# Cross attention in the third layer: value and output weights multiplied in an earlier stage, and the weighing done in f32r with high and low parts

## The chip, the core and the metric

One core of one Trainium2 chip runs the whole program, in one launch. The metric is the time on the device in microseconds (us), lower is better. Besides the timed runs there is one profiled execution; starts and durations below are from it, counted from the start of its span. The engines are TensorE (PE; its weight loads are PEld), VectorE (DVE), ScalarE (ACT), GpSimd (POOL) and SyncE (SP, which only issues transfers here).

## The reference, cut to what matters

The reference is a stack of transformer-like layers on 4 sequences of 256 tokens and 256 channels. The change touches two of its parts, the feed-forward part of the second layer (three 8-bit products with a GELU between them) and this cross attention of the third layer:

```python
q = (hidden_states @ Wq).reshape(B, Sq, H, D)            # B 4, Sq 256, H 16, D 128
k = (encoder_hidden_states @ Wk).reshape(B, Skv, H, D)   # the context has 128 channels
v = (encoder_hidden_states @ Wv).reshape(B, Skv, H, D)
q = rmsnorm(q, gq)
k = rmsnorm(k, gk)
scores = einsum('bqhd,bkhd->bhqk', q, k) * scale
attn = softmax(scores, axis=-1)
out = einsum('bhqk,bkhd->bqhd', attn, v)
return out.reshape(B, Sq, H * D) @ Wo
```

## The kernel before

The kernel keeps the residual `x_res` in SBUF and runs one stage after another. Every stage ends with a barrier of all engines. Within a stage each engine has its own instruction list in fixed order, and semaphores tie the lists together.

`l1_ffn` is the feed-forward stage of the second layer. Its main loop has 16 iterations n. PE makes two 128x512 products (`up`), ACT takes one of them and applies the GELU (`take`, L2691 and L2693), and DVE takes the other and multiplies (`product`, L2719 and L2724). ACT (`square`, L2344 to L2348), DVE and POOL then round the result to 8-bit values. `downward` runs behind it for half of the tokens at a time. `Norm` and `Turned` normalise and transpose the input ahead of the loop.

`l2_cross` is the changed stage. It never forms the values v. For each head h it multiplies the value and output weights into one 128x256 matrix, `wvo[:, h, :]`, and works as out = (attn · context) · wvo. Its main loop is a list of steps (it, s), with s from 0 to 15. In step (it, s) head s of sequence it - 1 goes through the pipeline, and the same step projects the keys and queries of sequence it (`pieces`): keys in s 0 to 3, queries in s 3 to 10, sums of squares and means in s 11, turned keys in s 12 to 15. The products of `wvo` (`outw`, L2978 on PE, L3067 on ACT) were pieces of pass it = 0, s 4 to 11; their inputs were loaded by `at_sp` after the stage's first barrier. I call a run of 16 steps with the same `it` a pass: pass 0 only prepares, passes 1 to 3 do both, and pass 4 only works on heads. Head number m = 16(it - 1) + s is what the steps are about:

```python
score(m)            # PE L2988, two f32 matmuls of 256 columns
turn_probs(m - 2)   # PE L2997, four f32 transposes
weigh(m - 3)        # PE L3008, two f32 matmuls of 256 columns
out_product(m - 4)  # PE L3019, the same with wvo; then the pieces of the step
```

On DVE a step is `largest(m)` (the row maximum, L3094, then the small bias for the exponential, L3096), `take_probs(m - 2)` (the copy out of PSUM, L3102), `invert(m)` (L3106), and then what the pieces need: copies of keys (L3120), of turned keys (L3157), `rescale` (L3149), sums. On ACT it is `exponent(m)` (two exponentials and the reads of their sums, L3046), `copy_out(m - 3)` (L3053), and for queries a copy and a square (L3061, L3063). On POOL it is `normalise(m)` (L3205), and in s 1 to 4 also `square` (L3201). `exponent(m)` waits for the bias of head m, `invert(m)` for its exponentials, `normalise(m)` for the reciprocal, and the bank pair 6 and 7 of PSUM alternates over all pieces, so a piece waits until the piece two before it has been taken.

In the profile one f32 matmul of the program shows as two PE records.

Of the kernel before, what the change touches and what calls it, by code (L numbers as in the profile page):

```python
# [2624 lines left out]
def l1_ffn(k):  # L2625
# [5 lines left out]
    with ExitStack() as cx:  # L2631
        sb = k.buffers(cx, "l1f_")
        w8, x8 = sb("w8", [P, 6144], BF16), sb("x8", [P, 2, TOK], F8)
        k.load("l1f", w8[:, :], k.kept8)
# [50 lines left out]
        def at_act():  # L2685
# [178 lines left out]
def l2_cross(k):  # L2864
# [16 lines left out]
    def pieces(b, s):
# [14 lines left out]
    def bank_free(*u):  # L2896
# [12 lines left out]
        return kt_sb(8 * b + i + 1) if kind == "turn" else vo_sb(i + 1)  # L2909

    with ExitStack() as cx:
        sb = k.buffers(cx, "l2x_")
# [20 lines left out]
        pr, pT, oT = sb("probs", [P, 3, 2, S]), sb("pT", [P, 2, 2, S]), sb("oT", [P, 2, S])  # L2933

        def at_pe():
            def piece(kind, b, i):
# [29 lines left out]
                elif kind == "turn":  # L2966
# [6 lines left out]
                else:  # L2973
                    if i == 0:
                        pe.wait_ge(*vo_in(2))
                    pe.wait_ge(*bank_free(kind, b, i))
                    for a in range(2):
                        last = pe.matmul(out[:, a * D:(a + 1) * D], wv[:, 2 * i + a, :], wo[:, 2 * i + a, :], start=True, stop=True)  # L2978
                    last.then_inc(*vo_ps.tick())
# [59 lines left out]
        def at_act():  # L3039
# [720 lines left out]
```

## Time and profile before

| | us |
|---|---|
| median of 3 runs | 2517.75 |
| lowest and highest | 2515.58, 2519.55 |
| the profiled execution's own time | 2513.59 |
| its span in the trace | 2512.4 |
| PE busy | 2084.8 (83%) |
| DVE busy | 1549.1 (62%) |
| ACT busy | 1086.3 (43%) |
| POOL busy | 1075.8 (43%) |
| `l1_ffn`, issue of its weights; main loop | 1242.7; 1250.6 to 1322.5 |
| `l2_cross`, first load to last statistics | 1674.6 to 2044.9 |

A busy share is an average over all stages. What the change does is to be read in the two stages that it touches, from which engine the others wait for there. The page's PE clock row is in tenths of full speed, and matmul ends are modelled, so for PE the distance from one start to the next tells more than a duration.

### The profile page before, as it was taken

Reading aid. Unit: us, or ns where it says so; the run is one execution under the profiler, and the core shown is the slowest. Engines: PE = TensorE matmul, PEld = TensorE weight load, DVE = VectorE, ACT = ScalarE, POOL = GpSimd, SP = SyncE. Lnnn points to the kernel's source line nnn. Section 1 sums busy time; section 2 is a strip of 40 time slices with the busy share of each in tenths; the row PEclk is TensorE's granted clock in tenths of the full one; section 3 lists DMA queues with packets and bytes.
Section 4 is the critical chain, followed back from the end, with each engine's and each line's share of the span. In section 5 each row is a group of like instructions: output and inputs, shape, how many; then the busy total and the mean of one; then the engine's idle time right before and its main releaser. Section 6 shows DMA issues by size and latency. Waiting matters only on the chain. (4 is left out here: it accounts for less than half of the span.)

```text
span 2512.4 us, 35632 instructions
## 1 busy us (share of the span) xinstructions
PE 2084.8 (83%) x12866; PEld 1427.6 (57%) x12866; DVE 1549.1 (62%) x2880; ACT 1086.3 (43%) x2193; POOL 1075.8 (43%) x1101
## 2 busy tenths in 40 slices
PE   5667769999966999968748888877999988898877
PEld 2333346666745999944514444545777765555445
DVE  6877755545455777757685555544456555556546
ACT  3245636455533544534271355532444434432433
POOL 2776707556647777647352233331223222231000
PEclk8766689999987999989859789888999999989788
DMA  4222210000005555430101000020000000112000
GB/s 146 70 61 61 60 43 20 24 13 12 10 23 186 183 181 180 156 128 1 50 1 39 3 3 3 3 110 0 1 1 1 1 1 2 36 42 107 2 1 17
DMA packets 49869, 124.53 MB, mean 50 GB/s; under 512 B 5632, under 2 KB 18432, under 8 KB 47520
## 3 DMA queue, kind: packets, MB, share of 16 engines
q1 hardware_dynamic: 48160, 118.07, 14.7%
q0 software_dynamic: 1536, 4.20, 0.5%
q8 instruction: 104, 1.70, 0.3%
q14 instruction: 69, 0.57, 0.1%
HBM read 105.07 MB, written 16.12 MB: 48 GB/s over the span
## 5 line engine op out<-in xcount | busy, mean ns | idle before, releaser
L1846 POOL TENSOR_SCALAR l0f_probs<-l0f_probs,l0f_tot 128x128 f32<-128x128 f32 (+1 forms) x256 | 202.6, 809 | 121.9 <-DVE l0f_tot L1793 121.6
L236 PE MATMUL ps<-kb 128*128 128x512 bf16 x524 | 149.7, 432 | 55.9 <-PEq L239 55.9
L3205 POOL TENSOR_TENSOR l2x_probs<-l2x_probs,l2x_rc 128x512 f32<-128x512 f32 x64 | 66.5, 1039 | 256.2 <-DVE l2x_rc L3106 256.2
L1308 DVE TENSOR_REDUCE l2a_a_max<-ps 128x6 f32<-128x768 f32 x128 | 119.5, 954 | 87.3 <-PE ps L1160 86.7
L1364 POOL TENSOR_SCALAR_AFFINE_SELECT l2a_a_probs<-l2a_a_probs 128x256 f32<-128x256 f32 (+1 forms) x192 | 88.3, 484 | 170.3 <-ACT l2a_a_probs L1270 147.9
L2064 PE MATMUL ps<-l0f_xh,l0f_wh 128*128 128x256 f32 x480 | 145.9, 304 | 0.0
L2181 POOL TENSOR_TENSOR l0f_wl<-l0f_raw,l0f_wh 128x1024 fp32r<-128x1024 f32 x60 | 142.1, 2388 | 0.0
L1717 ACT ACTIVATE l0f_probs<-ps,l0f_neg 128x128 f32<-128x128 f32 (+1 forms) x256 | 104.5, 425 | 78.6 <-DVE l0f_neg L1783 78.5
L2065 PE MATMUL ps<-l0f_xl,l0f_wh 128*128 128x256 f32 x480 | 136.0, 283 | 0.0
L2066 PE MATMUL ps<-l0f_xh,l0f_wl 128*128 128x256 f32 x480 | 136.0, 283 | 0.0
L3046 ACT ACTIVATE l2x_probs<-ps,l2x_neg,l2x_rs 128x256 f32<-128x256 f32 x128 | 71.1, 559 | 146.1 <-DVE l2x_neg L3096 146.1
L236 PEld LDWEIGHTS ps<-kb 128*128 128x128 bf16 x524 | 52.5, 106 | 124.8 <-issue 88.9
L701 DVE TENSOR_TENSOR_SCAN l1x_h<-l1x_dA,l1x_dBu 128x512 f32<-128x512 f32 x64 | 117.2, 1870 | 7.6 <-ACT l1x_dA L688 7.6
L719 POOL TENSOR_TENSOR l1x_y<-l1x_y,l1x_hc 128x512 f32<-128x512 f32 x64 | 80.8, 1284 | 87.6 <-DVE l1x_hc L710 87.6
L2077 PE MATMUL ps<-l0f_raw_d,l0f_gf 128*128 128x256 f32 x480 | 113.3, 379 | 0.0
L1007 POOL TENSOR_TENSOR l0x_y<-l0x_y,l0x_hc 128x512 f32<-128x512 f32 x64 | 80.3, 1275 | 44.5 <-DVE l0x_hc L980 44.3
L1308 DVE TENSOR_REDUCE l0a_max<-ps 128x4 f32<-128x1024 f32 x64 | 77.7, 1214 | 28.4 <-PE ps L1155 27.8
L2077 PEld LDWEIGHTS ps<-l0f_raw_d,l0f_gf 128*128 128x128 f32 x480 | 88.8, 190 | 9.9
L2064 PEld LDWEIGHTS ps<-l0f_xh,l0f_wh 128*128 128x128 f32 x480 | 92.3, 192 | 2.5
L2065 PEld LDWEIGHTS ps<-l0f_xl,l0f_wh 128*128 128x128 f32 x480 | 92.3, 192 | 1.1
L2066 PEld LDWEIGHTS ps<-l0f_xh,l0f_wl 128*128 128x128 f32 x480 | 92.1, 192 | 0.0
L1270 ACT ACTIVATE l2a_a_probs<-ps 128x1024 f32<-128x1024 f32 x64 | 65.7, 1027 | 58.9 <-PE ps L1187 58.4
(722 smaller groups left out, 5786.4 us busy)
## 6 DMA issues: line engine op xcount, KB each, us to landing
l0f_raw<-in_e_l0f SPq DMA_DIRECT2D x60, 512.0 KB, 4.1
l0x_bc<-scratch_bc SPq DMA_DIRECT2D x32, 512.0 KB, 4.8
l0f_raw_d<-in_e_l0f SPq DMA_DIRECT2D x60, 256.0 KB, 3.2
scratch_rows<-zero SPq DMA_DIRECT2D x1, 3840.0 KB, 19.0
l0f_xb<-scratch_rows SPq DMA_DIRECT2D x15, 256.0 KB, 3.0
scratch_results<-l0f_yb SPq DMA_DIRECT2D x15, 256.0 KB, 2.3
l2f_ew<-in_e_l2f SPq DMA_DIRECT2D x8, 384.0 KB, 3.1
l2f_raw<-in_w_l3f SPq DMA_DIRECT2D x1, 2304.0 KB, 10.3
```

What stands on the lines that cost most here:

```text
L236: self.pe.matmul(bank, self.identb, self.kb[:, 0:512], start=True, stop=True)
L701: k.dve.tensor_tensor_scan(self.row(self.h, d), self.row(self.dA, d), self.row(self.dBu, d), 0.0, ALU.mult, ALU.add).then_inc(*self.state. ...
L719: k.pool.tensor_tensor(yd, yd, self.row(self.hc, d), ALU.add).then_inc(*self.summed.tick())
L1308: dve.tensor_reduce(M[:, 2 * half:2 * half + 2, j, :], src.rearrange("p a (c n) -> p a c n", c=NB_), AX.X, ALU.max).then_inc(*unit_max.tick())
L1364: last = pool.affine_select(part, part, [[0, m], [1, P]], ALU.is_ge, 0.0, base=0, channel_multiplier=-1)
L1717: last = act.activation(pr[:, u % 4, a, r], ps[:, 2 * (u % 2) + a, r], ACT.Exp, scale=scale, bias=neg[:, u % 4, qt, a:a + 1], accum_out=to ...
L1846: last = pool.tensor_scalar(pr[:, u % 4, a, r], pr[:, u % 4, a, r], tot[:, u % 4, qt, a:a + 1], None, ALU.mult)
L2064: pe.matmul(out, hi, xh[:, j % 2, c, :], start=c == 0, stop=False)
L2065: pe.matmul(out, hi, xl[:, j % 2, c, :], start=False, stop=False)
L2066: last = pe.matmul(out, lo, xh[:, j % 2, c, :], start=False, stop=c == 1)
L2077: last = pe.matmul(ps[:, 4 + j % 2, q * D:(q + 1) * D], gf[:, n % 3, f * BLOCK + q * P:f * BLOCK + (q + 1) * P], raw_d[:, n % 6, f * D:(f ...
L2181: pool.tensor_tensor(wl[:, n % 3, :], raw[:, n % 4, :], wh[:, n % 3, :].bitcast(F32), ALU.subtract).then_inc(*w_lo.tick())
```

## The change

Three things. First, `wvo` becomes a buffer that is allocated before `l1_ffn`. That stage now loads the value and output weights (1 MB and 2 MB, behind its own weights on SP), and PE multiplies them in iterations 1 to 8 of its loop (`out_weights`), while ACT takes the results in iterations 2 to 9 (`take_out_weights`). The pieces `outw` and the two loads leave `l2_cross`. Second, the weighing product is made of six f32r matmuls instead of two f32 ones: high context by high probabilities, high by low, and low by high, for each half of the keys. Third, for this the turned probabilities are taken in two parts: ACT copies the high part out of PSUM (`high_probs`), and DVE, which used to copy, subtracts the high part from PSUM to get the low one. The context is split once, by ACT and POOL in pass 0.

```diff
@@ l1_ffn
         k.load("l1f", w8[:, :], k.kept8)
+        wv, wo = sb("wv", [P, 16, P]), sb("wo", [P, 16, D])
+        vo_in, vo_ps, vo_sb = k.sig("out0", 16), k.sig("vo_ps"), k.sig("vo_taken")
+        k.sp.dma_start(wv[:, :, :], k.dram["g_l2x"][:, 6144:8192].rearrange("p (h c) -> p h c", c=P)).then_inc(*vo_in.tick())
+        k.sp.dma_start(wo[:, :, :], k.dram["g_l2x"][:, 8192:12288].rearrange("p (h n) -> p h n", n=D)).then_inc(*vo_in.tick())
+        landed = vo_in.now()
...
+                elif t == 0:
+                    pe.wait_ge(*vo_sb(8))
...
+            def out_weights(i):
+                if i == 0:
+                    pe.wait_ge(*landed)
+                if i >= 2:
+                    pe.wait_ge(*vo_sb(i - 1))
+                for a in range(2):
+                    last = pe.matmul(ps[:, 6 + i % 2, a * D:(a + 1) * D], wv[:, 2 * i + a, :], wo[:, 2 * i + a, :], start=True, stop=True)
+                last.then_inc(*vo_ps.tick())
+
             for n in range(N):
                 up(n)
+                if 1 <= n <= 8:
+                    out_weights(n - 1)
...
+            def take_out_weights(i):
+                act.wait_ge(*vo_ps(i + 1))
+                act.copy(k.wvo[:, 2 * i:2 * i + 2, :].rearrange("p h n -> p (h n)"), ps[:, 6 + i % 2, :]).then_inc(*vo_sb.tick())
+
             for n in range(N + 1):
                 if n < N:
                     take(n)
                 if n:
                     square(n - 1)
+                if 2 <= n <= 9:
+                    take_out_weights(n - 2)
@@ l2_cross
-        return out + ([("outw", 0, s - 4)] if b == 0 and 4 <= s < 12 else [])
+        return out
...
-        xT, wk, wq, wvo = sb("xT", [P, 2, TOK]), sb("wk", [P, 2048]), sb("wq", [P, 2, 2048]), sb("wvo", [P, H, D])
+        xT, wk, wq, wvo = sb("xT", [P, 2, TOK]), sb("wk", [P, 2048]), sb("wq", [P, 2, 2048]), k.wvo
...
-        pr, pT, oT = sb("probs", [P, 3, 2, S]), sb("pT", [P, 2, 2, S]), sb("oT", [P, 2, S])
+        pr, oT = sb("probs", [P, 3, 2, S]), sb("oT", [P, 2, S])
+        ph, pl = sb("pT_h", [P, 2, 2, S], F32R), sb("pT_l", [P, 2, 2, S], F32R)
+        ch, cl = sb("ctx_h", [P, NT, DC], F32R), sb("ctx_l", [P, NT, DC], F32R)
...
-                for kt in range(2):
-                    last = pe.matmul(ps[:, 4, n % 2 * S:(n % 2 + 1) * S], ctx[:, 2 * b + kt, :], pT[:, n % 2, kt, :], start=kt == 0, stop=kt == 1)
+                for i, (c, p, kt) in enumerate([(c, p, kt) for kt in range(2) for c, p in ((ch, ph), (ch, pl), (cl, ph))]):
+                    last = pe.matmul(ps[:, 4, n % 2 * S:(n % 2 + 1) * S], c[:, 2 * b + kt, :], p[:, n % 2, kt, :], start=i == 0, stop=i == 5)
...
+            def high_probs(n):
+                act.wait_ge(*p_ps(n + 1))
+                if n >= 2:
+                    act.wait_ge(*product(n - 1))
+                act.copy(ph[:, n % 2, :, :].rearrange("p k s -> p (k s)"), ps[:, 2 + n % 2, :]).then_inc(*p_hi.tick())
+
...
                 if 0 <= m < N:
                     exponent(m)
+                if 0 <= m - 2 < N:
+                    high_probs(m - 2)
                 if 0 <= m - 3 < N:
                     copy_out(m - 3)
+                if it == 0 and s == 9:
+                    act.wait_ge(*c_in.now())
+                    act.copy(ch[:, :, :], ctx[:, :, :]).then_inc(*c_hi.tick())
...
             def take_probs(n):
-                dve.wait_ge(*p_ps(n + 1))
-                if n >= 2:
-                    dve.wait_ge(*product(n - 1))
-                dve.tensor_copy(pT[:, n % 2, :, :].rearrange("p k s -> p (k s)"), ps[:, 2 + n % 2, :]).then_inc(*p_sb.tick())
+                dve.wait_ge(*p_hi(n + 1))
+                dve.tensor_tensor(pl[:, n % 2, :, :].rearrange("p k s -> p (k s)"), ps[:, 2 + n % 2, :],
+                                  ph[:, n % 2, :, :].rearrange("p k s -> p (k s)").bitcast(F32), ALU.subtract).then_inc(*p_sb.tick())
...
+                if it == 0 and s == 9:
+                    pool.wait_ge(*c_hi(1))
+                    pool.tensor_tensor(cl[:, :, :], ctx[:, :, :], ch[:, :, :].bitcast(F32), ALU.subtract).then_inc(*c_lo.tick())
 
         def at_sp():
-            sp.dma_start(wv, k.dram["g_l2x"][:, 6144:8192].rearrange("p (h c) -> p h c", h=H)).then_inc(*vo_in.tick())
-            sp.dma_start(wo[:, :, :], k.dram["g_l2x"][:, 8192:12288]).then_inc(*vo_in.tick())
@@ build
+        k.wvo = k.buffers(ctx, "l2x_")("wvo", [P, 16, D])
         l1_ffn(k)
```

On ACT, in the last pass of `l2_cross`, the instruction list of before repeats these rows for each head (L3046 is the exponential, `l2x_oT` the copy of the weighed context):

```order
L3046 ACTIVATE l2x_probs,l2x_tot<-ps,l2x_neg,l2x_rs 128x256 [waits s_turned,s_bias]
L3046 ACTIVATE l2x_probs,l2x_tot<-ps,l2x_neg,l2x_rs 128x256
L3053 COPY l2x_oT<-ps 128x256 [waits s_out_ps,s_product]
L3046 ACTIVATE l2x_probs,l2x_tot<-ps,l2x_neg,l2x_rs 128x256 [waits s_turned,s_bias]
L3046 ACTIVATE l2x_probs,l2x_tot<-ps,l2x_neg,l2x_rs 128x256
```

The same place of the changed kernel:

```order
L3063 ACTIVATE l2x_probs,l2x_tot<-ps,l2x_neg,l2x_rs 128x256 [waits s_turned,s_bias]
L3063 ACTIVATE l2x_probs,l2x_tot<-ps,l2x_neg,l2x_rs 128x256
L3070 CAST l2x_pT_h<-ps 128x512 [waits s_product,s_turned]
L3076 COPY l2x_oT<-ps 128x256 [waits s_out_ps,s_product]
L3063 ACTIVATE l2x_probs,l2x_tot<-ps,l2x_neg,l2x_rs 128x256 [waits s_turned,s_bias]
```

The new cast stands behind both exponentials of the step, although it belongs to the head two before theirs.

On DVE at the same place, before:

```order
L3094 TENSOR_REDUCE l2x_mx<-ps 128x2 [waits s_scored]
L3096 SCALAR_TENSOR_TENSOR l2x_neg<-l2x_mx,l2x_rs 128x2 [waits s_v]
L3102 COPY l2x_pT<-ps 128x512 [waits s_product,s_turned]
L3106 RECIPROCAL l2x_rc<-l2x_tot 128x2 [waits s_weighed]
L3094 TENSOR_REDUCE l2x_mx<-ps 128x2 [waits s_scored]
```

And after:

```order
L3114 TENSOR_REDUCE l2x_mx<-ps 128x2 [waits s_scored]
L3116 SCALAR_TENSOR_TENSOR l2x_neg<-l2x_mx,l2x_rs 128x2 [waits s_v]
L3120 TENSOR_TENSOR l2x_pT_l<-ps,l2x_pT_h 128x512 [waits s_x_hi]
L3125 RECIPROCAL l2x_rc<-l2x_tot 128x2 [waits s_weighed]
L3114 TENSOR_REDUCE l2x_mx<-ps 128x2 [waits s_scored]
```

The order is the same; the third instruction now waits for ACT (`x_hi` is the semaphore of the cast), where it had waited for PE.

On PE at the start of the loop of `l1_ffn`, the changed kernel has these rows (before, the rows L2672 stood without those of L2691 between them):

```order
L2672 MATMUL ps<-l1f_x,l1f_w 128x512 [waits s_ld_l1f,barrier_Pool_Activation_PE_DVE_SP_release]
L2672 MATMUL ps<-l1f_x,l1f_w 128x512 x7
L2691 MATMUL ps<-l1f_wo,l1f_wv 128x256 [waits s_out0]
L2691 MATMUL ps<-l1f_wo,l1f_wv 128x256
L2672 MATMUL ps<-l1f_x,l1f_w 128x512 x4
```

Behind the products of iterations 0 and 1 PE now waits for the two new loads (`out0`), and the products of iteration 2 stand behind that wait.

## Rows read from the trace of the kernel before

**Rows 1.** Busy time by engine in stretches of `l2_cross`: setup, one pass, last pass.
```profile
core 0: us, PE busy (x) PEld busy (x) DVE busy (x) ACT busy (x) POOL busy (x), PEclk, DMA share, GB/s
...
1693.80:1713.80 20.00, 18.01 (x77) 13.98 (x78) 0.56 (x1) 9.87 (x20) 0.00 (x0) 1.00 0.00 1
...
1785.80:1869.50 83.70, 81.58 (x404) 64.02 (x403) 48.78 (x94) 35.04 (x100) 24.03 (x20) 1.00 0.00 1
...
1988.70:2042.70 54.00, 53.71 (x281) 46.66 (x279) 28.97 (x70) 25.86 (x85) 16.64 (x16) 1.00 0.00 1
```
**Rows 2.** Timeline of PE, one head of the last pass.
```profile
2012.03 0.60 PE L2997 MATMUL ps<-kf,l2x_probs 128*128 128x128 f32 x4
2012.46 1.03 PE L3008 MATMUL ps<-l2x_pT,l2x_ctx 128*128 128x256 f32 x4
2013.33 1.03 PE L3019 MATMUL ps<-l2x_wvo,l2x_oT 128*128 128x256 f32 x4
2014.19 1.03 PE L2988 MATMUL ps<-l2x_kT,l2x_qT 128*128 128x256 f32 x4
```
**Rows 3.** Timeline of DVE, the same head, and the next maximum.
```profile
2009.20 0.69 DVE L3094 TENSOR_REDUCE l2x_mx<-ps 128x2 f32<-128x512 f32 x1 [0.71 <-PE ps L2988]
...
2009.92 0.16 DVE L3096 SCALAR_TENSOR_TENSOR l2x_neg<-l2x_mx,l2x_rs 128x2 f32<-128x2 f32 x1
...
2011.36 0.17 DVE L3106 RECIPROCAL l2x_rc<-l2x_tot 128x2 f32<-128x2 f32 x1 [0.66 <-ACT l2x_probs L3046]
...
2012.23 0.69 DVE L3094 TENSOR_REDUCE l2x_mx<-ps 128x2 f32<-128x512 f32 x1 [0.70 <-PE ps L2988]
```
**Rows 4.** Timeline of ACT, same head: first exponential, then the copy behind both.
```profile
2010.12 0.56 ACT L3046 ACTIVATE l2x_probs<-ps,l2x_neg,l2x_rs 128x256 f32<-128x256 f32 x1 [1.56 <-DVE l2x_neg L3096]
...
2011.22 0.36 ACT L3053 COPY l2x_oT<-ps 128x256 f32<-128x256 f32 x1
```
**Rows 5.** Timeline of POOL, the same head.
```profile
2011.60 1.04 POOL L3205 TENSOR_TENSOR l2x_probs<-l2x_probs,l2x_rc 128x512 f32<-128x512 f32 x1 [1.99 <-DVE l2x_rc L3106]
```
**Rows 6.** Timeline of DVE, one step that turns keys, pass 1.
```profile
1813.05 0.68 DVE L3094 TENSOR_REDUCE l2x_mx<-ps 128x2 f32<-128x512 f32 x1
...
1815.19 0.17 DVE L3106 RECIPROCAL l2x_rc<-l2x_tot 128x2 f32<-128x2 f32 x1 [0.66 <-ACT l2x_probs L3046]
...
1815.28 1.39 DVE L3157 TENSOR_SCALAR l2x_kT<-ps,l2x_gg 128x512 f32<-128x512 f32 x2
...
1817.72 0.69 DVE L3094 TENSOR_REDUCE l2x_mx<-ps 128x2 f32<-128x512 f32 x1
```
**Rows 7.** Timeline of both engines where a bias meets a POOL instruction.
```profile
1745.98 1.89 POOL L3201 TENSOR_TENSOR l2x_sq<-l2x_k 128x1024 f32<-128x1024 f32 x1
...
1746.71 1.17 DVE L3096 SCALAR_TENSOR_TENSOR l2x_neg<-l2x_mx,l2x_rs 128x2 f32<-128x2 f32 x1
```
**Rows 8.** Groups by line and form, cross and feed-forward stages of the last layer.
```profile
L3594 ACT CAST l3f_xTh<-ps 128x512 fp32r<-128x512 f32 x2 | 1.2, 586 | 4.8 <-PE ps L393 4.8
...
L3598 DVE TENSOR_TENSOR l3f_xTl<-ps,l3f_xTh 128x512 fp32r<-128x512 f32 x4 | 2.5, 684 | 0.2 <-ACT l3f_xTh L3594 0.2
```
**Rows 9.** Timeline of PE, f32r matmuls of 256 columns in the first layer's experts.
```profile
903.57 0.28 PE L2066 MATMUL ps<-l0f_xh,l0f_wl 128*128 128x256 f32 x1
903.69 0.28 PE L2064 MATMUL ps<-l0f_xh,l0f_wh 128*128 128x256 f32 x1
```
**Rows 10.** Timeline of PE, two following query pieces of pass 0.
```profile
1701.07 1.99 PE L2950 MATMUL ps<-l2x_xT,l2x_wq 128*128 128x256 f32 x8 [0.31 <-ACT l2x_sq L3063]
...
1704.24 1.99 PE L2950 MATMUL ps<-l2x_xT,l2x_wq 128*128 128x256 f32 x8 [0.31 <-ACT l2x_sq L3063]
```
**Rows 11.** Timelines of DVE (first) and ACT (second), loop of `l1_ffn`.
```profile
1258.90 0.68 DVE L2719 CAST l1f_ub<-ps 128x512 bf16<-128x512 f32 x1
...
1268.35 0.63 ACT L2344 ACTIVATE l1f_I<-l1f_ab 128x512 f32<-128x512 bf16 x1 [0.78 <-DVE l1f_ab L2724]
```
**Rows 12.** DMA issues of the stage's start, KB each and us to landing.
```profile
l2x_wq<-in_g_l2x SPq DMA_DIRECT2D x1, 2048.0 KB, 9.5
```

More of the change, by code:

```diff
@@ L2872, in l2_cross @@
     scale = 1.0 / math.sqrt(hd)
-    k_in, q_in, vo_in, c_in = k.sig("slab0", 16), k.sig("slab1", 16), k.sig("out0", 16), k.sig("out1", 16)
+    k_in, q_in, c_in = k.sig("slab0", 16), k.sig("slab1", 16), k.sig("out1", 16)
     k_ps, k_sb, q_ps, q_sb, q_sq = k.sig("projected"), k.sig("k_taken"), k.sig("q_ps"), k.sig("q_taken"), k.sig("q_squared")
@@ L2908, in bank_free @@
             return mean(b + 1)
-        return kt_sb(8 * b + i + 1) if kind == "turn" else vo_sb(i + 1)
+        return kt_sb(8 * b + i + 1)
     with ExitStack() as cx:
         sb = k.buffers(cx, "l2x_")
-        xT, wk, wq, wvo = sb("xT", [P, 2, TOK]), sb("wk", [P, 2048]), sb("wq", [P, 2, 2048]), sb("wvo", [P, H, D])
+        xT, wk, wq, wvo = sb("xT", [P, 2, TOK]), sb("wk", [P, 2048]), sb("wq", [P, 2, 2048]), k.wvo
         ctx = sb("ctx", [P, NT, DC])
@@ L2965, in piece @@
                     last.then_inc(*rows_ps.tick())
-                elif kind == "turn":
+                else:
                     pe.wait_ge(*scaled(4 * b + i // 2 + 1))
@@ L2972, in piece @@
                     last.then_inc(*kt_ps.tick())
[L2973 to L2979, printed above, removed]
             def score(n):
@@ L3002, in weigh @@
                 if n == 0:
-                    pe.wait_ge(*c_in.now())
+                    pe.wait_ge(*c_lo(1))
                 pe.wait_ge(*p_sb(n + 1))
@@ L3056, in take_queries @@
                 act.wait_ge(*q_ps(8 * b + i + 1))
-                if b == 1 and i == 0:
-                    act.wait_ge(*vo_ps(8))
                 if b >= 2 and i == 0:
@@ L3063, in take_queries @@
                 act.activation(sq[:, 2 * i:2 * i + 2, :].rearrange("p h s -> p (h s)"), bank("queries", b, i), ACT.Square).then_inc(*q_sq.tick())
-            def take_out_weights(i):
-                act.wait_ge(*vo_ps(i + 1))
-                act.copy(wvo[:, 2 * i:2 * i + 2, :].rearrange("p h n -> p (h n)"), bank("outw", 0, i)).then_inc(*vo_sb.tick())
             def take_root(b):
@@ L3085, in at_act @@
                             take_root(b)
-                        elif kind == "outw":
-                            take_out_weights(i)
             k.root_table()
@@ L3154, in take_turned @@
                     dve.wait_ge(*scored(H * (b - 1)))
-                if b == 1 and i == 0:
-                    dve.wait_ge(*vo_ps(8))
                 dve.tensor_scalar(KT[b % 2][:, 2 * i:2 * i + 2, :].rearrange("p h s -> p (h s)"), bank("turn", b, i), gg[:, 0:1], None, ALU.mult).then_inc(*kt_sb.tick())
@@ L3212, in at_pool @@
                     square(it, s - 1)
+                if it == 0 and s == 9:
+                    pool.wait_ge(*c_hi(1))
+                    pool.tensor_tensor(cl[:, :, :], ctx[:, :, :], ch[:, :, :].bitcast(F32), ALU.subtract).then_inc(*c_lo.tick())
         def at_sp():
-            sp.dma_start(wv, k.dram["g_l2x"][:, 6144:8192].rearrange("p (h c) -> p h c", h=H)).then_inc(*vo_in.tick())
-            sp.dma_start(wo[:, :, :], k.dram["g_l2x"][:, 8192:12288]).then_inc(*vo_in.tick())
             for s in (k_in, q_in, c_in):
                 sp.wait_ge(*s.now())
-            sp.wait_ge(*vo_in.now())
         at_pe()
```

6 lines of the change are left out of this document (2 added, 4 removed).

## The prediction

> **What bounds the kernel now.** The change touches two stages, so I read those, not the whole span. First the busy time by stretch [rows 1]. In one full pass of `l2_cross` PE is busy 81.58 of 83.70 us, in the last pass 53.71 of 54.00, at full granted clock, and DVE about half. By this table PE is the limit. A table of shares hides how close the next limit is, so next I laid the timelines of one head side by side.
>
> In the last pass a head takes 3.03 us from one row maximum to the next [rows 3]. PE needs all of it: weighing starts at 2012.46, the output product at 2013.33, the next score at 2014.19, so 0.86 us for each pair of f32 matmuls, and 0.43 for the transposes [rows 2]. Beside it runs a chain that goes back and forth between DVE and ACT. The maximum starts at 2009.20, the bias at 2009.92 [rows 3], the first exponential at 2010.12, and ACT is free again at 2011.22 [rows 4]. The reciprocal starts at 2011.36 [rows 3]. From the maximum these are 0.72, 0.92, 2.02 and 2.16 us. DVE is then free 0.09 us later, as 1815.19 to 1815.28 shows [rows 6]. So the chain takes 2.25 us, 0.78 less than PE. The copy of the probabilities costs nothing there: DVE makes it while ACT computes exponentials.
>
> In a step that turns keys PE is not the limit even now. Maximum to maximum is 4.67 us, and DVE works through it: 2.14 to the reciprocal, then two turned keys and one rescaling [rows 6]. Any lengthening of the chain is paid there in full.
>
> **Setup: `outw` leaves pass 0.** Query pieces follow each other every 3.17 us, and PE waits at each for the square of the query piece before [rows 10]. With `outw` between them, queries always use the same PSUM bank. Without it they alternate over two, and the pitch becomes PE's own: eight half matmuls at 0.86/4 = 0.216, or 1.73 us. ACT needs less than that for a copy and a square, about 1.2 by the 0.59 of a cast of this form [rows 8]. Six pieces gain 6 x 1.44 = 8.6, and the first wait for the weights (pieces went on at 1693.8, the last sums began at 1713.8 [rows 1]) adds some tenths: **-9.0**. The split of the context is 1024 wide. It stands in step 9, where ACT has 0.5 us to spare per piece, and PE is a full piece ahead; twice the 512-wide cast is 1.2, so it delays one copy by some 0.6 and is caught up by the next. POOL is idle. Price 0; if its cover went, 0.6.
>
> **Weighing on PE.** Six f32r matmuls of 256 columns start 0.12 us apart [rows 9], so 0.72 instead of 0.86: -0.14 per head. It counts only where PE bounds the step, some seven query steps in each of passes 1 to 3: 21 x 0.14 = **-3.0**. If a change of type costs a start, the gain is nothing. The Trainium skill (TensorE: Matmul & The Clock Gate, "Wait — 56ns, not 53.3ns?") gives columns over 2.4 GHz plus about 2.5 ns, measured for bf16, as the distance of two matmuls. That would be 0.109 and a gain of 0.21 per head, -4.4 instead of -3.0. The row has the very type and shape, so its 0.12 stands.
>
> **The high and low parts.** The high part, an ACT cast of 128x512 from PSUM, takes 0.586 us, and the subtraction on DVE, one operand in PSUM, 0.684 [rows 8]. By duration the subtraction only replaces a copy of 0.69. By place it does not. The cast stands behind the exponentials of the step, the subtraction waits for it, and the reciprocal and the next maximum are queued behind the subtraction. So the hidden copy is now in series. The chain from the maximum: 2.02 until ACT is free, 2.61 cast done, 0.03 for the signal, 0.60 until DVE takes the next instruction, reciprocal at 3.24. That is **1.08 us later** than 2.16. The next maximum can start at 3.33.
>
> Bounds: if the cast cost only its pitch, near 0.49, the shift is about 1.0; with one more signal it is 1.2.
>
> Then POOL. Its normalisation starts 0.24 after the reciprocal and takes 1.04 us [rows 5]. The bias is short, 0.16 us, but where one met a POOL instruction it was stretched until that ended: started at 1746.71 against a POOL instruction from 1745.98 for 1.89, it took 1.17 [rows 7]. With the new chain this happens in the last pass at every head: normalisation from 3.48 to 4.52, the next bias due at 3.33 + 0.72 = 4.05, so it ends near 4.7, and a head takes 4.54 - 0.72 = **3.82** instead of 3.03.
>
> Now the places, one by one:
> - last pass: 14 heads x 0.79 = 11.1; the head with the residual addition and the end of the pipeline (cast and subtraction once more) together 1.7: **+12.8**
> - steps that turn keys, and the one behind them (also bound by DVE, since its keys follow the reciprocal): 5 steps x 3 passes x 1.08 = **+16.2**
> - the step that takes the roots, and the one before it, where the chain starts late: some 0.6 per pass, **+2**
> - key steps: the chain, 3.33 + 2 x 0.6 for the keys, just about equals PE. But POOL's 1.89 us square starts when the keys are copied, near 4.7, and the next bias falls into it, as in rows 7. That costs 1.1, twice a pass: **+6.6**
> - query steps: chain 3.33, PE 4.6. The chain is hidden; only the -3.0 counts.
>
> The loop comes to 12.8 + 16.2 + 2 + 6.6 - 3.0 = +34.6.
>
> **`l1_ffn`.** SP issues 3 MB behind the stage's 1.5 MB. A load of 2048 KB, with 1024 KB of another in front of it, landed 9.5 us after its issue [rows 12]. Scaled by 4608/3072 KB that is 14.2 us, and the stage issues at 1242.7: landing near 1257. PE reaches the wait two iterations into a loop that starts at 1250.6, long before. Iteration 2 is queued behind: after the wait four half matmuls and its own four products, 1.7 to 3.4 us by the clock. DVE took its product at 1258.90 [rows 11], so it comes 0 to 3 us late; I take 1.5. The eight copies of 0.59 on ACT: ACT waits 0.78 us for DVE in an iteration [rows 11], so they fit: 0, and 8 x 0.59 = 4.7 without that cover. Term: **+1.5**, bounds 0 and 7.
>
> **Sum.** -9.0 + 34.6 + 1.5 = +27.1 us, so 2513.6 becomes 2540.7 for a profiled execution. That execution was 4.2 us under the median of runs; added to the median, 2517.75 + 27.1 = 2544.9. I say **2545**.
>
> **The rivals.**
> - *The bias does not wait for POOL, or only sometimes.* A head of the last pass takes 3.33, not 3.82 (-6.9), and key steps lose the 6.6: +13.6, 2531. For it: the chain may settle in another phase. Against it: the bias is due 0.5 us after POOL starts, every time. The Trainium skill (SBUF — State Buffer, "Practical consequences") says that a DVE instruction with two SBUF inputs contends with a GpSimd one that reads SBUF, and the loser blocks for the whole instruction. By that rule the wait is no accident; the 1.17 us row agrees. Chance 0.12.
> - *The feed-forward stage pays more.* ACT becomes its limit and the wait for 3 MB is long: +7 instead of 1.5, 2550. For it: the wait comes while the loop fills, when every engine needs PE. Against it: the 0.78 us that ACT has to spare once it runs. Chance 0.14.
> - *Faster: PE stays the limit.* If cast and subtraction hid in the 0.78 us that the chain is shorter than PE, and the turning steps grew no longer, the change keeps -9.0, the 0.14 at all 64 heads (-9.2), and +1.5: -16.7, 2501. It decides at a lengthening of about 0.3 us a step: 15 steps on DVE's path times 0.3, with 1 us elsewhere, make up for what is saved. I forecast 1.08 from measured durations and a fixed order. Chance 0.05.
> - *Gain and loss cancel.* The chain grows by some 0.4 and the net is within 5 us: 2517. Chance 0.03.
>
> **How the numbers follow.** My forecast has 0.66; its own range, from a shift of 1.0 to 1.2 over some 35 steps, 0 to 3 us in `l1_ffn` and 4 us between runs, is 2538 to 2552. Reaching to the two rivals on the slow side gives 2531 to 2554, with some 0.12 outside. A measurement of this kernel tells 0.2% (5 us) from no change. Faster by over that 0.05, within it 0.03, slower 0.92.
>
> **What would show it.** In the changed trace: query pieces of pass 0 some 1.73 us apart and the first row maximum near 9 us earlier within the stage; the subtraction on DVE idle before it, released by ACT's cast; maximum to maximum 3.8 in the last pass and 5.75 in turning steps; biases of 0.6 us instead of 0.16; weighing 0.72 us on PE, with PE idle behind it; the first product of the new pair in `l1_ffn` waiting for a DMA. Wrong would be: 3.0 in the last pass (the cast is hidden), 3.3 (no wait for POOL), or a loop of `l1_ffn` longer by over 4 us.

## The result

The changed kernel takes 2548.68 us (median of 4 runs, 2545.38 to 2554.99), the kernel before 2516.66 us (median of 4 runs beside them). The ratio is 1.0121, 95% interval 1.0095 to 1.0147: by the ratio 30.5 us slower, interval 24 to 37; the medians differ by 32. The forecast was 2545 us, range 2531 to 2554.

The profiled execution took 2545.38 us with a span of 2544.1, against 2513.59 and 2512.4. I cut both spans at the same instructions:

| stretch, from start to start | before | after | difference |
|---|---|---|---|
| `l1_ffn`: main loop to POOL's last product | 65.38 | 67.29 | +1.9 |
| `l2_cross`: first keys to the sums of pass 0 | 32.30 | 23.19 | -9.1 |
| `l2_cross`: first row maximum to the last | 294.29 | 325.72 | +31.4 |
| `l2_cross`: last maximum to the next stage | 11.75 | 12.59 | +0.8 |
| the rest, whose code didn't change | 2108.64 | 2115.33 | +6.7 |

One head of the last pass after the change, the timeline of DVE, ACT and POOL alone (start, us, engine, line, and in brackets the idle time before it and what ended it):

```profile
2035.93 0.58 ACT L3070 CAST l2x_pT_h<-ps 128x512 fp32r<-128x512 f32 x1
2036.54 0.69 DVE L3120 TENSOR_TENSOR l2x_pT_l<-ps,l2x_pT_h 128x512 fp32r<-128x512 f32 x1 [1.75 <-ACT l2x_pT_h L3070]
2037.15 0.15 DVE L3125 RECIPROCAL l2x_rc<-l2x_tot 128x2 f32<-128x2 f32 x1
2037.22 0.67 DVE L3114 TENSOR_REDUCE l2x_mx<-ps 128x2 f32<-128x512 f32 x1
2037.38 1.04 POOL L3222 TENSOR_TENSOR l2x_probs<-l2x_probs,l2x_rc 128x512 f32<-128x512 f32 x1 [2.60 <-DVE l2x_rc L3125]
2037.92 0.52 DVE L3116 SCALAR_TENSOR_TENSOR l2x_neg<-l2x_mx,l2x_rs 128x2 f32<-128x2 f32 x1
2038.47 0.56 ACT L3063 ACTIVATE l2x_probs<-ps,l2x_neg,l2x_rs 128x256 f32<-128x256 f32 x1 [1.69 <-DVE l2x_neg L3116]
2039.57 0.58 ACT L3070 CAST l2x_pT_h<-ps 128x512 fp32r<-128x512 f32 x1
2040.18 0.69 DVE L3120 TENSOR_TENSOR l2x_pT_l<-ps,l2x_pT_h 128x512 fp32r<-128x512 f32 x1 [1.74 <-ACT l2x_pT_h L3070]
2040.79 0.15 DVE L3125 RECIPROCAL l2x_rc<-l2x_tot 128x2 f32<-128x2 f32 x1
2040.86 0.67 DVE L3114 TENSOR_REDUCE l2x_mx<-ps 128x2 f32<-128x512 f32 x1
```

Read it against [rows 3, 4], and against the copy of the turned probabilities in the same head of the kernel before, from its timeline:

```profile
2010.00 0.69 DVE L3102 COPY l2x_pT<-ps 128x512 f32<-128x512 f32 x1
```

Maximum to maximum is now 3.64 us. The copy stood beside ACT's exponentials (2010.12 to 2011.22); the subtraction in its place waits 1.74 us for the cast, which starts when the second exponential is done, and the reciprocal and the next maximum follow at once. POOL starts 0.16 us behind the maximum, and the bias, 0.16 us long before, takes 0.52: it ends at 2038.44, POOL at 2038.42. ACT waits 1.69 us for it.

In the key steps the bias meets POOL's square, as in [rows 7] but now twice in every pass. From the timeline of a pass 2 step:

```profile
1840.71 1.89 POOL L3218 TENSOR_TENSOR l2x_sq<-l2x_k 128x1024 f32<-128x1024 f32 x1
1840.74 0.68 DVE L3114 TENSOR_REDUCE l2x_mx<-ps 128x2 f32<-128x512 f32 x1
1841.45 1.17 DVE L3116 SCALAR_TENSOR_TENSOR l2x_neg<-l2x_mx,l2x_rs 128x2 f32<-128x2 f32 x1
```

The delay goes on to PE, and now and then to its clock. PE's timeline in pass 2, and windows of the same place in passes 1, 2 and 3 (columns as in [rows 1]):

```profile
1845.78 2.62 PE L2976 MATMUL ps<-l2x_xT,l2x_wq 128*128 128x256 f32 x8 [2.59 <-DVE l2x_k L3139]
1848.19 1.91 PE L3007 MATMUL ps<-l2x_kT,l2x_qT 128*128 128x256 f32 x4
```

```profile
1756.00:1760.00 4.00, 4.00 (x20) 3.42 (x19) 1.96 (x3) 1.22 (x3) 0.69 (x1) 0.72 0.00 0
...
1846.00:1850.00 4.00, 4.00 (x13) 3.14 (x13) 3.85 (x5) 1.08 (x2) 2.10 (x2) 0.62 0.00 0
...
1937.00:1941.00 4.00, 3.82 (x22) 3.46 (x23) 3.96 (x6) 1.18 (x2) 2.51 (x2) 1.00 0.02 4
```

Behind its wait of 2.59 us PE was granted 0.62 in pass 2, a part of the time at 1.2 GHz, and made 13 matmuls in 4 us; four of a score took 1.91 instead of 1.03. In pass 3, behind an equal wait but at 2.4 GHz throughout, it made 22. In pass 1 the wait was 3.40 us, and the clock was down behind it too. The step of the long wait and the next took 9.61 and 4.60 us in pass 1, 9.40 and 4.82 in pass 2, 9.06 and 3.46 in pass 3; before, 6.86 and 4.76, then twice 8.07 and 3.36.

Of the 64 biases 23 are longer than 0.23 us after the change, 6 before. Each of the 23 ends 0.02 us behind a POOL instruction. Of the two long ones in the key steps of pass 1 neither is new: the kernel before has both, and [rows 7] shows the first. The page's costliest groups show who pays (busy and mean ns, then idle time before and its releaser):

```profile
L3222 POOL TENSOR_TENSOR l2x_probs<-l2x_probs,l2x_rc 128x512 f32<-128x512 f32 x64 | 66.6, 1040 | 267.9 <-DVE l2x_rc L3125 267.9
L3063 ACT ACTIVATE l2x_probs<-ps,l2x_neg,l2x_rs 128x256 f32<-128x256 f32 x128 | 71.0, 559 | 162.7 <-DVE l2x_neg L3116 162.6
L3120 DVE TENSOR_TENSOR l2x_pT_l<-ps,l2x_pT_h 128x512 fp32r<-128x512 f32 x64 | 44.2, 691 | 108.4 <-ACT l2x_pT_h L3070 108.4
```

The last row is the new wait: 108.4 us over 64 heads, 1.69 each. Most of it is idle time that DVE had anyway, now in another place, so it is not the loss itself; the next section tells what of it is.

In `l1_ffn` the timeline shows the wait for the 3 MB, and the window behind it the clock:

```profile
1258.11 2.07 PE L2691 MATMUL ps<-l1f_wo,l1f_wv 128*128 128x256 f32 x4 [4.24 <-DMA l1f_wo<-in_g_l2x]
1261.08 0.58 ACT L2709 CAST l1f_gb<-ps 128x512 bf16<-128x512 f32 x1 [2.86 <-PE ps L2672]
1261.93 0.69 DVE L2743 CAST l1f_ub<-ps 128x512 bf16<-128x512 f32 x1 [1.57 <-PE ps L2672]
```

```profile
1258.00:1262.00 4.00, 3.89 (x9) 2.43 (x10) 1.07 (x3) 1.11 (x3) 2.53 (x2) 0.50 0.00 0
```

PE comes out of the wait at a granted clock of 0.50, that is 1.2 GHz, and the four matmuls of the fold take 2.07 us. DVE's product of iteration 2 starts 9.94 us into the loop (from 1251.99), before 8.29 (1258.90 [rows 11] less 1250.61): 1.65 later.

### The profile page after: what moved, and what is told of

It is laid out like the page before. It is cut to its first block and busy times, and to the rows that moved or that the text cites. A ratio compares the mean times of both kernels' runs of the same rounds, so it can differ in the third digit from the quotient of the medians.

```text
span 2544.1 us, 35890 instructions
## 1 busy us (share of the span) xinstructions
PE 2078.2 (82%) x12933; PEld 1435.7 (56%) x12994; DVE 1550.9 (61%) x2880; ACT 1116.9 (44%) x2258; POOL 1078.6 (42%) x1102
## 5 line engine op out<-in xcount | busy, mean ns | idle before, releaser
L236 PE MATMUL ps<-kb 128*128 128x512 bf16 x493 | 144.0, 437 | 60.3 <-PEq L239 44.4
L3120 DVE TENSOR_TENSOR l2x_pT_l<-ps,l2x_pT_h 128x512 fp32r<-128x512 f32 x64 | 44.2, 691 | 108.4 <-ACT l2x_pT_h L3070 108.4
```

Of the source, the lines that this page charges most:

```text
L236: self.pe.matmul(bank, self.identb, self.kb[:, 0:512], start=True, stop=True)
```

## The experiments

Ten kernels ran, each beside the kernel before. "Heads" is the time from the first row maximum to the last in the profiled execution; "last" and "turning" are maximum to maximum in the last pass and in a step that turns keys.

| kernel | median us | ratio to before, 95% | heads | last | turning |
|---|---|---|---|---|---|
| before | 2516 to 2517 | | 294.3 | 3.03 | 4.67 |
| changed | 2548.68 | 1.0121 (1.0095 to 1.0147) | 325.7 | 3.64 | 5.74 |
| fold_only | 2511.38 | 0.9974 (0.9957 to 0.9990) | 294.3 | 3.03 | 4.67 |
| hilo_only | 2550.04 | 1.0128 (1.0103 to 1.0152) | 325.9 | 3.65 | 5.74 |
| high_first | 2506.20 | 0.9953 (0.9936 to 0.9970) | 288.4 | 2.87 | 4.67 |
| invert_first | 2530.36 | 1.0052 (1.0036 to 1.0069) | 310.6 | 3.23 | 5.68 |
| both_first | 2519.11 | 1.0004 (0.9985 to 1.0023) | 299.7 | 2.87 | 5.27 |
| bias_scalar | 2537.62 | 1.0084 (1.0062 to 1.0107) | 318.5 | 3.46 | 5.92 |
| high_late | 2500.78 | 0.9944 (0.9921 to 0.9967) | 288.4 | 2.87 | 4.67 |
| best | 2509.25 | 0.9965 (0.9947 to 0.9983) | 289.6 | 2.87 | 4.84 |
| two_products | 2488.51 | 0.9901 (0.9869 to 0.9932) | 273.2 | 2.57 | 4.67 |
| after_again | 2552.02 (one run) | | 327.4 | 3.65 | 5.74 |

### The two halves of the change apart

**fold_only** takes the weighing back to f32 and one copy on DVE, and leaves out the cast and the split of the context (in part):

```diff
...
-                for i, (c, p, kt) in enumerate([(c, p, kt) for kt in range(2) for c, p in ((ch, ph), (ch, pl), (cl, ph))]):
-                    last = pe.matmul(ps[:, 4, n % 2 * S:(n % 2 + 1) * S], c[:, 2 * b + kt, :], p[:, n % 2, kt, :], start=i == 0, stop=i == 5)
+                for kt in range(2):
+                    last = pe.matmul(ps[:, 4, n % 2 * S:(n % 2 + 1) * S], ctx[:, 2 * b + kt, :], pT[:, n % 2, kt, :], start=kt == 0, stop=kt == 1)
...
-                dve.tensor_tensor(pl[:, n % 2, :, :].rearrange("p k s -> p (k s)"), ps[:, 2 + n % 2, :],
-                                  ph[:, n % 2, :, :].rearrange("p k s -> p (k s)").bitcast(F32), ALU.subtract).then_inc(*p_sb.tick())
+                dve.tensor_copy(pT[:, n % 2, :, :].rearrange("p k s -> p (k s)"), ps[:, 2 + n % 2, :]).then_inc(*p_sb.tick())
```

> The changed kernel with its weighing put back to f32 and one copy of the turned probabilities on DVE; the folding stays in the second layer's experts. Theory A (the loss is the cast and the subtraction in series before the reciprocal, and the fold by itself gains): 9 us less in l2_cross ahead of the heads, 1.5 to 2.5 us more in the experts, heads as in the kernel before (3.03 us in the last pass, 4.7 where keys are turned), so about 2509 to 2512 us, 5 to 8 below before. Theory B (the fold costs too: its 3 MB of loads, its copies on ACT and the 32 KB of a partition that stay taken make stages around it slower): at or above before, 2517 to 2523 us, with the 5 us that stages with unchanged code lost still there.

**hilo_only** is the kernel before with the weighing and its casts of the changed one; `outw` stays in pass 0.

> The kernel before with the weighing in f32r with high and low parts alone; the output weights are folded in l2_cross as before. Theory A: the heads carry the whole loss, so about 34 us more than before, 2548 to 2554 us, with heads of the last pass at 3.6 to 3.8 us and turning steps at 5.7, and the experts as before. Theory B (a good part of the 32 us is the fold's or the placement's): 2535 to 2545 us.

The fold alone is 6.5 us faster (interval 2.5 to 10.8): 23.16 us from keys to sums instead of 32.30, and 66.99 in `l1_ffn`'s loop instead of 65.38, together -7.5. The high and low parts alone are 32.2 us slower, and their heads take what the changed kernel's take, within 0.2 us. Theory A holds for both. The heads carry the loss: 31.6 us of it in hilo_only, beside 1.6 in its pass 0, where PE waited 2.51 us for the weights instead of 0.92. The fold doesn't touch the heads.

### Added work, or its place

**high_first** exchanges two calls on ACT; **invert_first** two on DVE, in the changed kernel; **both_first** does both:

```diff
 # high_first, ACT
+                if 0 <= m - 2 < N:
+                    high_probs(m - 2)
                 if 0 <= m < N:
                     exponent(m)
-                if 0 <= m - 2 < N:
-                    high_probs(m - 2)
 # invert_first, DVE
+                if 0 <= m < N:
+                    invert(m)
                 if 0 <= m - 2 < N:
                     take_probs(m - 2)
-                if 0 <= m < N:
-                    invert(m)
```

> The changed kernel with one exchange on ACT: the cast of the head two back stands ahead of the exponentials of this head instead of behind them. Nothing is taken away, all the work of the high and low parts stays. Theory A (the loss is a place in the order: the cast waits behind the exponentials, the subtraction for the cast, the reciprocal and the next maximum behind that): the chain falls apart, PE sets the head again with its shorter weighing, last pass 2.8 to 3.0 us a head, turning steps back to about 4.7, in all some 40 us below the changed kernel and 5 to 15 below before: 2500 to 2512 us. Theory B (the loss is the added work itself: 0.58 us of cast on ACT and six f32r matmuls on PE in each head): at most 10 us below the changed kernel, 2538 us or more. Theory C (the exchange only moves the wait, since the exponentials now start later and the bias is off the chain): 2515 to 2535 us.

> The changed kernel with one exchange on DVE: the reciprocal stands ahead of the subtraction. Theory A: the reciprocal no longer waits for the cast, so POOL's normalise starts earlier, but the subtraction and with it the next maximum still wait for the cast behind the exponentials; a part of the loss comes back: about 16 us below the changed kernel, 2528 to 2536 us, last pass 3.2 to 3.4 us a head. Theory B (the added work is the loss): no change, 2545 to 2552 us. A result as that of the exchange on ACT (2500 to 2512) would say that the reciprocal's place alone was the loss.

> Both exchanges at once: the cast ahead of the exponentials on ACT, and the reciprocal ahead of the subtraction on DVE. Theory A (what counts is that DVE's 0.7 us of the turned probabilities runs while ACT makes exponentials, not how early the reciprocal comes): the subtraction, ready early, now stands behind a reciprocal that waits for the exponentials, so the next maximum comes some 0.6 us later than with the cast first alone. PE still sets the last pass (2.9 us a head), but turning steps go from 4.67 to about 5.2, 15 of them: 8 to 12 us above the version with the cast first, about 2514 to 2519 us. Theory B (each exchange takes away a wait of its own and the gains add): below 2506 us.

With the cast first, all of the new work is still there and the kernel is 11.8 us faster than before (interval 7.5 to 16). The timeline of a head of its last pass:

```profile
2019.48 0.59 ACT L3070 CAST l2x_pT_h<-ps 128x512 fp32r<-128x512 f32 x1 [0.92 <-PE ps L3016]
2019.77 0.16 DVE L3116 SCALAR_TENSOR_TENSOR l2x_neg<-l2x_mx,l2x_rs 128x2 f32<-128x2 f32 x1
2019.97 0.57 ACT L3063 ACTIVATE l2x_probs<-ps,l2x_neg,l2x_rs 128x256 f32<-128x256 f32 x1
2020.10 0.69 DVE L3120 TENSOR_TENSOR l2x_pT_l<-ps,l2x_pT_h 128x512 fp32r<-128x512 f32 x1 [0.17 <-ACT l2x_pT_h L3070]
2021.20 0.17 DVE L3125 RECIPROCAL l2x_rc<-l2x_tot 128x2 f32<-128x2 f32 x1 [0.41 <-ACT l2x_probs L3063]
2021.92 0.69 DVE L3114 TENSOR_REDUCE l2x_mx<-ps 128x2 f32<-128x512 f32 x1 [0.55 <-PE ps L3007]
```

The cast starts 0.49 us ahead of the exponential, which still starts 0.04 us behind the end of the bias, as in the kernel before; so the cast delays it by nothing. The subtraction waits 0.17 us instead of 1.74 and lies beside the exponentials, and the maximum is now released by PE. With the order the new waits of the bias go too: 6 of the 64 are long, as before the change. Theory B, that the added work is the loss, and theory C, that the wait only moves, are out.

With the reciprocal first the changed kernel gets back a part, as expected: heads 310.6, and 3.23 us a head in the last pass. Its rows say why not more: the subtraction still waits for the cast, and the maximum for it.

```profile
2044.52 0.58 ACT L3070 CAST l2x_pT_h<-ps 128x512 fp32r<-128x512 f32 x1
2044.65 0.17 DVE L3125 RECIPROCAL l2x_rc<-l2x_tot 128x2 f32<-128x2 f32 x1 [1.27 <-ACT l2x_probs L3063]
2045.13 0.69 DVE L3120 TENSOR_TENSOR l2x_pT_l<-ps,l2x_pT_h 128x512 fp32r<-128x512 f32 x1 [0.31 <-ACT l2x_pT_h L3070]
2045.73 0.68 DVE L3114 TENSOR_REDUCE l2x_mx<-ps 128x2 f32<-128x512 f32 x1
```

Both exchanges together do not add up: 299.7, 11.3 us more than the cast first alone. A turning step takes 5.27 in place of 4.67, and the timeline of such a step shows DVE idle for 1.27 us behind the bias, with its 0.67 us subtraction, ready all the time, queued behind the reciprocal:

```profile
1825.26 0.16 DVE L3116 SCALAR_TENSOR_TENSOR l2x_neg<-l2x_mx,l2x_rs 128x2 f32<-128x2 f32 x1
1826.69 0.17 DVE L3125 RECIPROCAL l2x_rc<-l2x_tot 128x2 f32<-128x2 f32 x1 [1.27 <-ACT l2x_probs L3063]
1826.77 0.67 DVE L3120 TENSOR_TENSOR l2x_pT_l<-ps,l2x_pT_h 128x512 fp32r<-128x512 f32 x1
```

So what counts is that DVE's 0.6 to 0.7 us for the turned probabilities runs while ACT computes exponentials. The median, 2519.11, is just above the expected 2514 to 2519.

### The bias beside POOL

**bias_scalar** is the changed kernel with the bias in a form that takes one operand as numbers per partition:

```diff
-                dve.scalar_tensor_tensor(neg[:, n % 3, :], mx[:, n % 3, :], -1.0, rs[:, b % 2, 1, :, h], ALU.mult, ALU.mult).then_inc(*bias_ok.tick())
+                for qt in range(2):
+                    last = dve.tensor_scalar(neg[:, n % 3, qt:qt + 1], mx[:, n % 3, qt:qt + 1], rs[:, b % 2, 1, qt, h:h + 1], -1.0, ALU.mult, ALU.mult)
+                last.then_inc(*bias_ok.tick())
```

> The changed kernel with the bias written as two operations, one for each query tile, that each read one operand from SBUF and take the scale as a number per partition, in place of one operation with two operands from SBUF. Nothing else moves. Theory A (the bias waits for POOL's normalise and squares because both of its operands come from SBUF, and through the exponentials the head waits with it): biases of 0.1 to 0.2 us each, last pass 3.3 to 3.4 us a head in place of 3.64, key steps back to 4.8 and 8.1 or so, about 12 to 15 us below the changed kernel: 2531 to 2538 us. Theory B (any operation of DVE waits while POOL works, or the bias only shows a wait that the head would have anyway): no change, 2545 to 2552 us. If the new form still waits, the durations of the bias show it.

Its last pass in the timeline, POOL at work throughout the pair of biases:

```profile
2020.64 0.67 DVE L3114 TENSOR_REDUCE l2x_mx<-ps 128x2 f32<-128x512 f32 x1
2020.80 1.04 POOL L3224 TENSOR_TENSOR l2x_probs<-l2x_probs,l2x_rc 128x512 f32<-128x512 f32 x1 [3.80 <-DVE l2x_rc L3127]
2021.34 0.34 DVE L3117 TENSOR_SCALAR l2x_neg<-l2x_mx,l2x_rs 128x1 f32<-128x1 f32 x2
2021.71 0.56 ACT L3063 ACTIVATE l2x_probs<-ps,l2x_neg,l2x_rs 128x256 f32<-128x256 f32 x1 [1.51 <-DVE l2x_neg L3117]
```

And all of them, the summary of the line:

```profile
L3117 DVE TENSOR_SCALAR l2x_neg<-l2x_mx,l2x_rs x128: 202/208/215, 1737.5 to 2056.1; 128x1 f32<-128x1 f32 x128
```

The same summary of the changed kernel and its old form:

```profile
L3116 DVE SCALAR_TENSOR_TENSOR l2x_neg<-l2x_mx,l2x_rs x64: 160/163/1171, 1737.7 to 2063.4; 128x2 f32<-128x2 f32 x64
```

58 of the 128 overlap a POOL instruction and the longest takes 0.215 us. So the old form's waits are for POOL, as the forecast had it, and not those of DVE as such (theory B is out). The size was off. I had expected 0.1 to 0.2 us for the pair; it takes 0.34, 0.18 more than one free bias. So the last pass comes to 3.46 instead of 3.3 to 3.4, and each turning step pays 0.18. The key steps get back 6.5 us, the last pass 1.9, the query steps 1.3, and the steps from the roots to the end of the turning lose 2.6: heads 7.2 us shorter, where 12 to 15 were expected. A part of the 6.5 and all of the 1.3 are the clock: in this kernel no score behind the key steps is at the lower one. In pass 3, where the changed kernel kept its clock too, steps 1 to 4 get back 1.5 us together; in passes 1 and 2, where it did not, 3.2 each.

### What PE costs once it sets the pace

**two_products** is high_first with only the product of both high parts, so it computes less: the products with the low context and the low probabilities are missing.

```diff
-                for i, (c, p, kt) in enumerate([(c, p, kt) for kt in range(2) for c, p in ((ch, ph), (ch, pl), (cl, ph))]):
+                for i, (c, p, kt) in enumerate([(c, p, kt) for kt in range(2) for c, p in ((ch, ph),)]):
...
```

> The version with the cast first, but the weighing leaves out the four products with low parts: only the high context by the high probabilities is multiplied, two f32r matmuls in place of six. The cast, the subtraction and all waits stay. Theory A (with the cast first PE sets the pace, and an f32r matmul of 256 columns costs it 0.12 us): 0.48 us less in each head that PE bounds: last pass 2.4 us in place of 2.88, query steps 4.1 in place of 4.60, turning steps unchanged at 4.67 since DVE sets them; some 16 to 18 us below the version with six products, 2488 to 2493 us. Theory B (the chain of DVE and ACT is what leaves 2.88): last pass stays at 2.8 to 2.9.

Query steps go from 4.60 to 4.13, so four f32r matmuls cost 0.47, 0.12 each. Turning steps stay. The last pass goes to 2.57, not 2.40, between theory A and theory B; its timeline shows the next limit, the bias that meets POOL's normalise again:

```profile
2007.20 1.04 POOL L3222 TENSOR_TENSOR l2x_probs<-l2x_probs,l2x_rc 128x512 f32<-128x512 f32 x1 [1.53 <-DVE l2x_rc L3125]
2007.44 0.59 ACT L3070 CAST l2x_pT_h<-ps 128x512 fp32r<-128x512 f32 x1 [0.26 <-PE ps L3016]
2007.75 0.51 DVE L3116 SCALAR_TENSOR_TENSOR l2x_neg<-l2x_mx,l2x_rs 128x2 f32<-128x2 f32 x1
2008.30 0.56 ACT L3063 ACTIVATE l2x_probs<-ps,l2x_neg,l2x_rs 128x256 f32<-128x256 f32 x1 [0.26 <-DVE l2x_neg L3116]
```

PE is the limit of high_first in its last pass, but by 0.3 us only.

### Folding later, and the stages that didn't change

**high_late** is high_first with the folding two iterations later; **best** has the new bias in addition.

```diff
-                if 1 <= n <= 8:
-                    out_weights(n - 1)
+                if 3 <= n <= 10:
+                    out_weights(n - 3)
...
-                if 2 <= n <= 9:
-                    take_out_weights(n - 2)
+                if 4 <= n <= 11:
+                    take_out_weights(n - 4)
```

> The version with the cast ahead of the exponentials, with the folding two iterations later in the experts (products in iterations 3 to 10, copies in 4 to 11). Theory A (the 1.6 to 2.0 us that the experts' loop lost are the wait for the 3 MB of weights in iteration 1): that wait goes, the loop takes 65.4 to 66.0 us in place of 67.3, and the whole 2504 to 2507 us, hardly to be told from the 2506 of the version without it; the verdict is the loop's time. Theory B (the loss is the copies on ACT, which fill its iterations): the loop stays at 67.0 to 67.5 us.

> Cast ahead of the exponentials, folding two iterations later, and the bias in two operations with one SBUF operand each. With the cast first, the bias already starts behind POOL's normalise in the last pass (0.16 us long), so theory A expects only the few key steps to gain: 0 to 3 us below the version without the new bias, 2500 to 2506 us. Rival: the second small operation of DVE makes turning and query steps longer by its 0.06 us, so no gain or 2 us of loss.

> The changed kernel once more, for the stages whose code didn't change. If the 5.6 us that the third layer's stage of experts behind the heads and the 3.1 us that the second self attention took more in the first profile are the change's doing (a buffer's place, a clock phase), they stand again: about 263 and 353 us. If they are differences between executions, they come out at other values, within 255 to 263 and 349 to 367 us, while the heads take 325.7 us again within 0.5.

The loop of `l1_ffn` takes 65.95 us instead of 67.32, so 1.4 of the 1.9 us were the wait for the weights. Timeline and window of high_late:

```profile
1257.26 1.13 PE L2691 MATMUL ps<-l1f_wo,l1f_wv 128*128 128x256 f32 x4 [2.49 <-DMA l1f_wo<-in_g_l2x]
```

```profile
1257.00:1260.00 3.00, 2.74 (x13) 1.98 (x14) 1.61 (x4) 2.90 (x6) 1.66 (x2) 1.00 0.00 0
```

A wait of 2.49 is left in front of the first product, but two more iterations are done by then, and PE comes out of it at the full clock. How the 1.4 us divide into wait and clock these runs don't tell. Some 0.6 us against the kernel before stay. The eight copies may be the cause; no run shows it.

high_late is the fastest version with the whole computation, 14.1 us (8 to 20) below before, not to be told from high_first. best loses: heads 1.2 us longer, as its rival said. The new bias removes waits in key steps but costs 0.17 in each turning step.

after_again answers for the stages with unchanged code. The second self attention, which is the stage between the two that the change touches, took 352.74 us in the changed kernel's first profile and 357.01 in this one, 349.66 to 367.40 over all the profiled executions. The third layer's experts behind `l2_cross` took 263.07 and 259.47, and 255.32 to 264.11 over all. Windows of that stage show what goes with it. First the changed kernel, then high_late (columns as in [rows 1]):

```profile
2075.00:2338.00 263.00, 226.78 (x1264) 142.75 (x1270) 144.91 (x343) 91.87 (x134) 73.37 (x93) 0.90 0.09 31
```

```profile
2033.00:2289.00 256.00, 217.99 (x1270) 135.24 (x1268) 144.44 (x343) 91.70 (x134) 73.01 (x94) 0.94 0.09 32
```

DVE, ACT and POOL are busy for the same time; PE for 8.8 us more at a granted clock of 0.90 than at 0.94. fold_only, with the same buffer placed early, took 255.91. So those microseconds are differences between executions, not the change's doing. The heads of after_again took 327.4, outside the expected 325.7 within 0.5. PE was at the lower clock behind the key steps of all three passes, in the first profile of passes 1 and 2 alone: one more time some 1.7 us (9.37 + 4.86 in pass 3 against 9.06 + 3.46).

## Why the prediction was right

| term | forecast | measured |
|---|---|---|
| setup of pass 0 | -9.0 | -9.1 |
| last pass and pipeline's end | +12.8 | +10.3 |
| turning steps and those around the roots | +18.2 | +16.2 |
| key steps | +6.6 | +7.1 |
| query steps | -3.0 | -1.4 |
| `l1_ffn` | +1.5 | +1.9 |
| sum | +27.1 | +25.0 |

- **Setup**: -9.1 for -9.0; from the fifth query piece of pass 0 on they stand 1.73 us apart, as forecast, and 1.79 to 1.83 before it.
- **The chain's shift of 1.08 us** came out as 1.07 in the turning steps (5.74 less 4.67). high_first shows that it was the place of the cast. This step carried the forecast.
- **The bias waits for POOL**: right, shown by bias_scalar; the rival that it doesn't is out. The size for the last pass was too large: 3.64 a head, not 3.82. I let the bias run its 0.16 us after POOL's end; it ends 0.02 after it. 14 heads x 0.18 = 2.5 us, the miss of that line. The page "SBUF — State Buffer" of the Trainium skill says under "Practical consequences" that a DVE instruction with at most one SBUF input, outside the two-port modes, does not contend with GpSimd. The 128 short biases agree.
- **Steps around the roots**: I gave them 2 us; the step behind the last query pays 0.5 in all. The turning steps and the one behind them came to 15.7 for 16.2.
- **Key steps**: that 7.1 is close to 6.6 is partly luck. Two long biases a pass stand there as forecast, but in pass 1 the kernel before had both already, so that pass did not pay the forecast's 2.2 for them. In pass 3, where PE kept its clock, the three steps cost 1.5 and not 2.2. And PE lost its clock behind the key steps of passes 1 and 2, which was not in the forecast: the three steps cost 1.8 in pass 2, and 3.8 in pass 1, of which these runs don't tell how much is the clock.
- **Query steps**: PE's gain was there, 0.16 a step (4.76 to 4.60; forecast 0.14), but in pass 2 the step behind the key steps took 4.82 us, 1.4 more than the 3.46 of pass 3, where PE kept its clock. Without that the term would be -2.7. high_first, which kept its clock in all three passes, has -3.3 there.
- **`l1_ffn`**: the wait for 3 MB, forecast at 0 to 3 us late and taken as 1.5, was 1.65, a part of it the lower clock behind it. That the eight copies on ACT cost nothing is not shown: 0.6 us of the loop stay open.
- **The rival "faster"** needed the cast hidden. It is what high_first does: -11.8 where the rival had -16.7. It had counted the f32r gain at all 64 heads; turning steps, which DVE sets, don't get it (4.67 both times). The 0.3 us a step at which I let the sign turn does not add up: 15 x 0.3 and 1 are 5.5, and my terms save 9.0 + 3.0 - 1.5 = 10.5, so by them it turns near 0.6. both_first is the case: its turning steps are 0.60 longer, and it comes out level with the kernel before (1.0004).

The single misses also made up for each other: -2.5 in the last pass and -2.0 in the turning steps and around the roots, against +0.5, +1.6 and +0.4 elsewhere. The medians differ by 32 us and the touched stretches by 25. Most of the 7 between them lie in the stages of the table's last line, which differ as much between executions of one kernel; the interval of the median, 24 to 37, holds the 25.

## What to carry to other kernels

When work is moved from one engine to another, ask where in that engine's order it stands, and who is queued behind the one that now waits: with the same work in both, the kernel took 2548.7 us with the cast behind the exponentials and 2506.2 with it ahead of them. Work whose inputs are ready early (two heads back, here) is to be tried ahead of the instruction that waits for this step's result, on both engines; exchanging two such instructions is a cheap experiment. A wait that the old cycle never met, as the small bias beside POOL's products, comes with a new phase: lay the other engines' times beside the new cycle before trusting a duration.

## What the runs showed of the hardware

- A DVE operation of one element per partition that takes its second operand as a number per partition took 0.208 us, 0.13 from the start of one to the start of the next, beside POOL as without it (58 of 128 overlapped, longest 0.215). The form with two tensors from SBUF took 0.16 alone and up to 1.17 beside POOL, and all 23 long ones then ended 0.02 us after POOL (0.015 to 0.018).
- PE left a wait of 4.24 us for a DMA at a granted clock of 0.50 (1.2 GHz), and so it did in the other kernels with the fold in iterations 1 to 8 (waits of 3.83 to 4.40); in high_late and best, with waits of 2.49 and 2.46 us for the same weights, it left at 1.00. Behind equal waits of 2.59 us in key steps of the changed kernel it was granted 0.62 in pass 2 and 1.00 in pass 3. In bias_scalar, invert_first and high_first, whose longest key steps are shorter (in passes 2 and 3 8.2, 8.0 and 7.9 us where the changed kernel has 9.4 and 9.1), no score behind them was at the lower clock.
- The granted clock of unchanged code differed between executions of kernels that differ elsewhere: 0.90 or 0.94 in the same stage, 263 or 256 us; in the second self attention hilo_only was granted 0.78 in a stretch where the kernel before had 0.89, and that stage took 367.4 us instead of 349.7.
